# A graph network with a mixture-of-experts layer: all MLP units ahead of the matrix gather, row-major scans, output chunks loaded earlier, 36 columns by matmul in the last chunks

## The reference

```
x = x + gnn(layernorm(x))                       # 6250 nodes of 256, 200000 edges sorted by dst
    # relu(xn @ W + segment_sum((xn @ M)[src], dst))
x = x + ffn(layernorm(x))                       # 131072 edges, unsorted
    h      = x @ W_gat                          # 4 heads x 4 experts = 16 numbers per node
    e      = leaky_relu(a_src[src] + a_dst[dst])
    alpha  = exp(e - segment_max(e, dst)) / segment_sum(exp(...), dst)
    scores = layernorm(segment_sum(h[src] * alpha, dst) + b_gat).mean over heads
    w      = softmax(top 2 of the 4 scores), 0 for the others
    out    = sum over the 4 experts of w[e] * (gelu(x @ W1[e] + b1[e]) @ W2[e] + b2[e])
```

## Time and profile before

| what | before |
|---|---|
| time, median of 3 runs | 3039.76 us (3037.41 to 4880.14) |
| profiled execution, device time | 3039.66 us |
| its span, first to last instruction | 3038.4 us |
| mean granted TensorE clock | 0.921 of full |
| busy: PE, DVE, POOL | 2402.1, 2252.1, 2200.3 us |
| first stage, POOL's gathers | 63.8 to 2147.4 us, 1611 of them |
| second stage, POOL's gathers | 2188.8 to 2881.7 us, 512 of them |
| second stage, blocks picked | 2232.3 to 2871.1 us, 128 of them |
| POOL's last feature gather to the end | 155.7 us |

### The profile page before, as it was taken

The page is one execution under the profiler, slowest core; times in us unless marked ns, Lnnn a source line. Parts: engine busy times, 40 slices in busy tenths (PEclk is TensorE's granted clock), DMA queues, the critical chain, the costliest instruction groups (busy, mean ns, idle before and its releaser), DMA issues. The chain is left out here.

```text
span 3038.4 us, 42695 instructions
## 1 busy us (share of the span) xinstructions
PE 2402.1 (79%) x13244; PEld 1878.2 (62%) x13244; DVE 2252.1 (74%) x6360; ACT 541.7 (18%) x938; POOL 2200.3 (72%) x2260
## 2 busy tenths in 40 slices
PE   1466887878877878879888888988789999999723
PEld 0344565655655556557666666656579988888713
DVE  6589878877887656577666666666367999999958
ACT  4000121112112333322111111111100110011112
POOL 3677777777777777777777777777777777777760
PEclk9777998989999999989999999999899999999957
DMA  8977777777777777768877777877612222222188
GB/s 270 331 231 217 227 226 225 221 228 226 231 226 235 237 240 233 225 214 256 251 240 247 240 250 241 251 243 236 183 30 49 68 66 52 68 65 62 45 265 261
DMA packets 477160, 600.92 MB, mean 198 GB/s; under 512 B 72654, under 2 KB 415750, under 8 KB 474886
## 3 DMA queue, kind: packets, MB, share of 16 engines
q1 hardware_dynamic: 378886, 376.33, 37.6%
q0 software_dynamic: 97600, 220.02, 26.2%
q10 hardware_dynamic: 448, 1.85, 0.2%
HBM read 312.82 MB, written 286.79 MB: 197 GB/s over the span
## 5 line engine op out<-in xcount | busy, mean ns | idle before, releaser
L1544 POOL DMA_INDIRECT ring<-xn_d,srci x1611 | 1576.8, 979 | 514.5 <-issue 452.5
L776 DVE SCALAR_TENSOR_TENSOR ring<-ring,same_v,wide 128x256 f32<-128x256 f32 x1610 | 770.0, 478 | 564.1 <-PE wide L1352 460.0
L1352 PE MATMUL wide<-ring,one_hot 128*128 128x256 f32 x3222 | 916.5, 420 | 281.9 <-DMA ring<-xn_d,srci 171.4
L1352 PEld LDWEIGHTS wide<-ring,one_hot 128*128 128x128 f32 x3222 | 641.0, 208 | 514.6 <-DMA ring<-xn_d,srci 210.9
L1579 POOL DMA_INDIRECT g<-tab_d,srt x512 | 507.0, 990 | 156.1 <-issue 153.4
L1454 PE MATMUL wide<-tab_parts,low_hot 128*128 128x208 bf16 x6144 | 565.1, 253 | 50.3 <-DVE low_hot L818 50.2
L1454 PEld LDWEIGHTS wide<-tab_parts,low_hot 128*128 128x128 bf16 x6144 | 545.8, 98 | 71.2 <-DVE low_hot L818 63.4
L1410 PE MATMUL wide<-w2s,hh 128*128 128x256 f32 x1568 | 386.8, 391 | 1.5 <-DVE yo L754 1.5
L1400 PE MATMUL wide<-xt,w1s 128*128 128x512 f32 (+1 forms) x832 | 387.2, 589 | 0.8 <-DVE feat L744 0.8
L713 DVE TENSOR_SCALAR one_hot<-iota_f,dloc 128x128 f32<-128x128 f32 x1611 | 361.9, 304 | 3.2
L1157 ACT ACTIVATE hh<-wide,b1c 128x512 f32<-128x512 f32 (+1 forms) x208 | 137.9, 663 | 1215.7 <-PE wide L1400 1215.3
(11 more groups left out here) (359 smaller groups left out, 1444.2 us busy)
## 6 DMA issues: line engine op xcount, KB each, us to landing
run_d<-ring SPq DMA_DIRECT2D x201, 1024.0 KB, 5.3
ring<-xn_d,srci POOLq DMA_INDIRECT x1611
y_d<-yo SPq DMA_DIRECT2D x196, 128.0 KB, 2.6
comb<-y_d SPq DMA_DIRECT2D x28, 896.0 KB, 11.6
low_row<-low_d SPq DMA_DIRECT2D x16, 1024.0 KB
sum_d<-g SPq DMA_DIRECT2D x16, 768.0 KB, 3.9
g<-tab_d,srt POOLq DMA_INDIRECT x512
xn_d<-ring SPq DMA_DIRECT2D x7, 896.0 KB, 5.2
```

The lines of the kernel that those rows point to most:

```text
L776: dve_at["run", j] = step(V.scalar_tensor_tensor(out=o, in0=ring[:, (j - 1) // JC % RING, (j - 1) % JC, :], scalar=same_v[:, j:j + 1], in1 ...
L1352: T.matmul(wide[:, 4 + j // 2 % 2, j % 2 * D:(j % 2 + 1) * D], one_hot[:, j // 4 % 4, j % 4, :], ring[:, j // JC % RING, j % JC, :], start ...
L1544: G.indirect_dma_start(out=ring[:, s, j % JC, :], out_offset=None, in_=xn_d, in_offset=at_rows(srci[:, j:j + 1])).then_inc(sem(f"gather{s} ...
```

## The change

The diff has eight parts.

1. All of the 56 left units go ahead of the matrix steps: 8 of them (`GAP_UNITS`) into the first stage's loop at `gap_chunk` = 204, ahead of the turning of tile 48's sums, and 48 at the start of the second stage. The table is split between these units on DVE.
2. The last three chunks (13 to 15) have 36 columns by matmul and 28 by POOL: 131 blocks and 500 gathers instead of 128 and 512.
3. `weigh` and `sum_up` use row-major tiles: `by_row`, `logit`, `fade`, `reset_c`, each [128, rows, 65], column 0 of each row a restart value. One scan of 260 numbers makes all four maxima, five make the 20 sums. ACT copies the results back to `g` (six copies a chunk) before they are stored.
4. The end of the sort, one step before, is cut in five (`ENDS` = 4 more).
5. The zero stores and weight loads of c = 3 are spread: `run_d` at 3, `tab_d` at 4 and 5, `start_d` at 9 to 12, weights one at a time at 9 to 16.
6. Output chunk 0 and three of the loads of chunk 1 are loaded at matrix step 40; the rest of 1, and 2, after the last block is picked.
7. Part 1's gate stands ahead of output chunk 2's place in DVE's list; all seven tiles of chunk 2 are mixed by PE and ACT. Tiles by PE: 2, 2, 7, 3, 2, 3, 2 instead of 2 each.
8. The last store of sums is issued by ACT instead of SP.

```diff
+    gap_chunk = ready(NT - 1) + 3
+    units_at_visits, units_1 = units_1, units_1 + GAP_UNITS
-    turns_2, paced = ["unit"] * min(FIRST_UNITS, left), 0.0
-    (40 units spread over the matrix steps)
+    turns_2 = ["unit"] * left + ["matrix"] * matrix_total
...
 # PE, in the loop over c (ACT, DVE and SP likewise)
+            if c == gap_chunk:
+                for _ in range(GAP_UNITS):
+                    next(mlp)
             for k in due(c, 3):
                 turn_sums(k)
...
 # DVE, weigh(c)
-            for h in range(HEADS):
-                step(V.tensor_tensor_scan(g[:, s, :, FE + h], reset_c[:, c % 2, :], g[:, s, :, HX + h],
-                                          -BIG if c == 0 else before_top[:, :, h], ALU.add, ALU.max))
+            then(V.tensor_tensor(logit[:, :, now], g[:, s, :, HX:FE].rearrange("p k h -> p h k"),
+                                 a_dest.rearrange("p k h -> p h k"), ALU.add))
+            dve_at["topped", c] = then(V.tensor_tensor_scan(
+                flat(rows_top), flat(reset_c[:, :, :]), flat(logit[:, :, :]), 0.0, ALU.add, ALU.max))
 # DVE, sum_up(c)
-            for h in range(HEADS):
-                o = g[:, s, :, h * NX:(h + 1) * NX]
-                step(V.tensor_tensor(o, o, g[:, s, :, HX + h:HX + h + 1].broadcast_to([P, FC, NX]), ALU.mult))
-            for f in range(FE):
-                step(V.tensor_tensor_scan(g[:, s, :, f], st[:, :, h], g[:, s, :, f], ...))
+            for e in range(NX):
+                step(V.tensor_tensor(by_row[:, e * HEADS:(e + 1) * HEADS, now],
+                                     g[:, s, :, 0:HX].rearrange("p k (h e) -> p e h k", e=NX)[:, e, :, :],
+                                     rows_e[:, :, now], ALU.mult))
+            for e in range(NX + 1):
+                rows = flat(by_row[:, e * HEADS:(e + 1) * HEADS, :])
+                step(V.tensor_tensor_scan(rows, flat(fade[:, :, :]), rows, 0.0, ALU.mult, ALU.add))
...
 # SP, second stage
+            if done == PRELOAD:
+                (waits for x1_out, y_done, gelus, y_out)
+                for e in range(NX + 1):
+                    load_rows(0, e)
+                for e in range(EARLY_ROWS):
+                    load_rows(1, e)
...
 # DVE, output
-                if c * XG == t0:
+                if c == GATE_AT[part]:
                     gate(part, t0, t1)
-            s = c % CR
+            s, n = c % CR, XG - PE_TILES[c]
```

More of the change, by code:

```diff
@@ L311, in build @@
     PARTS = ((0, PART * XG), (PART * XG, NT))
+    first_mixed = [sum(PE_TILES[:c]) for c in range(NLN + 1)]
+    assert len(PE_TILES) == NLN and PE_TILES[PART - 1] == XG and GATE_AT == (0, PART - 1)
     FIX_PARTS = tuple((a, min(a + 512 // FG, NT)) for a in range(0, NT, 512 // FG))
-    ZERO_OUT = 16 * (FS + 3)
+    STARTS_ZERO, TABLE_ZERO = 16 * FS, 16 * 2
+    ZERO_AT, WEIGHTS_AT = 4, 9
+    GAP_UNITS = 8
     SHIFTED, SMALL, SCORES = 0, 64, 256
@@ L762, in vector_program @@
         for c in range(NCH + AFTER):
+            if c == gap_chunk:
+                for _ in range(units_1 - sum(late_after)):
+                    next(mlp)
             for k in due(c, 4):
@@ L788, in vector_program @@
                     norm_layer(k)
-        for _ in range(units_1 - sum(late_after)):
-            next(mlp)
         def split_table():
@@ L897, in weigh @@
+            then(V.tensor_tensor(logit[:, :, now], logit[:, :, now], rows_top[:, :, now], ALU.subtract))
+            dve_at["weighed", c] = then(V.tensor_scalar(fade[:, :, now], fade[:, :, now], 0.0, None, ALU.min))
             yield
@@ L938, in vector_program @@
         matrix_steps, chunks, done = matrix_gathers(), chunk_steps(), 0
-        for turn in turns_2:
+        table = split_table()
+        for i, turn in enumerate(turns_2):
             if turn == "unit":
                 next(mlp)
+                if 2 <= i:
+                    next(table, None)
                 continue
+            for _ in table:
+                pass
             next(matrix_steps)
@@ L1139, in sort_steps @@
                 yield
-            yield
+            for _ in range(ENDS + 1):
+                yield
             for t in range(NT):
@@ new lines, in scalar_program @@
+        for c in range(NLN):
+            if c == 0:
+                for _ in gate(0, *PARTS[0]):
+                    pass
+                A.wait_ge(dve_step, dve_at["gates", 0])
+            if c == PART:
+                A.wait_ge(dve_step, dve_at["gates", 1])
+            A.wait_ge(sem(f"comb_in{c % CR}"), 16 * (NX + 1) * (c // CR + 1))
+            tiles = range(XG - PE_TILES[c], XG)
+            if c == GATE_AT[1]:
+                second = gate(1, *PARTS[1])
+                for k in tiles:
+                    diagonals(c, k)
+                    if k in (2, 4, 6):
+                        next(second)
+                    if k >= 2:
+                        pour(c, k - 2)
+                for k in tiles[XG - 2:]:
+                    pour(c, k)
+                continue
+            for k in tiles:
+                diagonals(c, k)
+            for k in tiles:
+                pour(c, k)
@@ L1319, in sort_steps @@
                 yield
+            for _ in range(ENDS):
+                yield
             T.wait_ge(dve_step, dve_at["next"])
```

345 lines of the change are left out of this document (204 added, 141 removed).

## The result

| what | before | after |
|---|---|---|
| time, median of 4 runs | 3038.59 us (3036.72 to 3039.76, and one of 4880.14) | 3067.07 us (3056.04 to 3073.59) |
| profiled execution, device time | 3039.66 us | 3056.04 us |
| its span | 3038.4 us | 3054.8 us |
| last visit gather | 2147.4 us | 2129.0 us |
| first and last feature gather | 2188.8, 2881.7 us | 2186.9, 2865.7 us |

The ratio after to before is 1.0089, with a 95% interval of 1.0077 to 1.0102: the change makes the kernel 0.9% slower. 3034 was predicted, with a range of 3006 to 3057; the median lies 10 us above it. The execution of 4880.14 us is left out of the ratio, and no trace of it is kept. The profiled execution is the quickest of the four of after, so its trace explains 16.4 of the 28.5 us between the medians.

The account below looks back on a forecast made before the run. The prediction took POOL as the first stage's chain and DVE as the second stage's limit, with POOL close. From 3039.7 us, -14 + 21.4 + 0.3 - 13.0 = -5.3 gave 3034 us, range 3006 to 3057.

Parts of the forecast that it names:

- Spread stores and the cut sort: First stage: shorter POOL waits for the `run_d` store and the sort's last step, -14 us, bounds 0 and -14.7.
- The eight units: Between the stages: eight units ahead of tile 48 wait for `xt` and delay tile 48's features by 19.7 us.
- Rival B: Between the stages: `xt` lands early, tile 48 is not delayed, all of 19.7 goes: 3014 us; chance 0.08.
- Rival C: Second stage: POOL is the bound, with cheaper scans and full-rate column reads: 3017 us; chance 0.17.
- step "Blocks": Second stage: 131 blocks, 35.6 us a chunk including 1.0 for packed steps; scores of chunk 15 at 2903, +21.4 to L879.
- The row-major form: Chunk work on DVE: long scans save 3.1, column reads cost 0.9, restart columns 0.3: 13.5 becomes 11.6 us a chunk.
- DVE idle for PE for more than 2 us a chunk: Second stage, chunk steps: a sign that, if seen, would show the prediction wrong.
- products above 0.6: Chunk work on DVE: a sign that, if seen, would show the prediction wrong.
- step "Tail": After POOL's first tail gather: less mixing on DVE -11.8, part 1's gate wait +0.5, fewer loads -1.7: -13.0 us.
- From the logits to POOL's first tail gather: Stretch before the tail: scans and products -2.3, ACT's last copy +0.6, store beside seven loads +2: +0.3 us.
- D: Chunk work on DVE: dearer long scan (0.82) and column reads (0.3) make the kernel slower, 3058 us; chance 0.13.
- E: POOL stops as often as before, or the last store lands behind seven loads: 8 to 14 lost, 3046 us; chance 0.12.

Follow-up runs that it names:

- few_after2: Changed kernel with 1 feature gather a chunk by POOL, second run: 36.4 us a chunk, of it 1.9 DVE's wait for PE.
- few_unpack: Changed kernel with 1 feature gather a chunk and its row-major chunk work laid over 29 of 29 steps: 34.5 us a chunk.
- few_old_rows: Changed kernel with 1 feature gather a chunk and the chunk work of the kernel before, over 27 of 29 steps: 35.5 us a chunk.
- best: Changed kernel without units ahead of tile 48, most units among blocks, in-order products, chunk work over 29 steps, earlier x1 loads, other PE tiles: 4363.77 us, ratio 0.9916.
- best2: Kernel of best with tiles by PE 1, 1, 7, 3, 2, 3, 2: ratio to the kernel before 0.9892, on another chip 0.9920 (4310.60 us).
- old_rows: Changed kernel with the chunk work of the kernel before (24 scans of 64, no copies by ACT): 4406.96 us, ratio 1.0004 to the kernel before.
- start_only: Kernel before with only the spread zero stores and weight loads and the sort's end in five steps: 4394.26 us, ratio 0.9985.

## Why the prediction was wrong

**Right.** Spread stores and the cut sort: -14 predicted, -18.4 measured. POOL has no wait for `run_d` left in its first 400 us, where it had 9.0, and none above 0.3 between 900 and 1000. Over all visits its waits for `run_d` fell from 16.0 to 6.3 and those for DVE's running sums from 33.8 to 29.3, together 14.2; the other 4 us show in no wait, and in *after* all of this stands in one trace. The eight units: features +19.7 predicted. Relative to the last visit, POOL's first feature gather moved from 41.4 to 57.9 us, +16.5; on the other chips it lies 67 us (64 to 72, six runs) behind without the eight units and 87 (80 to 94, seven runs) with them (kernels with all their gathers). Rival B is out. Blocks start +42.1, against +42.9. Rival C is out: POOL ended 33 us ahead.

**Wrong, step "Blocks": packing, and DVE's own time.** A chunk takes 36.8, not 35.6. The trace of *after* splits this into 35.3 of DVE's own time, where my sum had 34.6, and 1.5 of waiting for PE, where I took 1.0 for the packing. Without the gathers packing costs even 1.9 (few_after2 against few_unpack), more than my bound of 1.7. Of the 3.5 x 1.1 = 3.9 us that DVE has to spare in the steps without chunk work, I counted on 2.9 to be saved by the two buffers; 1.9 to 2.4 are. The two errors are 0.5 + 0.7 = 1.2 us a chunk, 18 us in 15 chunks. The ledger lacks only 14.8, since I had counted 15.2 chunks up to the scores of chunk 15, where there are 15 (-6), and the first scores stand 96.4 us behind the first block and not 94 (+2). My own sign for it, DVE idle for PE for more than 2 us a chunk, stayed silent; the other, products above 0.6, came true.

**Within DVE's own time.** The row-major form was to save 13.5 - 11.6 = 1.9 and saves 1.0 (few_old_rows against few_unpack). A column read costs 0.71 - 0.355 = 0.36 more per instruction, not 0.18: 1.8 a chunk, not 0.9. I had taken the price from a reduction in steps of 16 bytes, and the steps here are of 96: 0.7 ns an element there, 1.4 here. The Trainium skill (SBUF — State Buffer, section Door 1: The DMA port swizzle) says that every new 16-byte line pays. The trace agrees that such reads pay, and the old products, four in a line, did not: 416 ns, as L903 over `step_f` in order, 0.42 us. The Trainium skill gives no size. A scan of 260 costs 0.61, close to the 0.65 taken, and six give 0.2 back; the last 0.2 of the 0.9 that are missing is not traced. Against this, the units that left the blocks free 0.7 a chunk and not the 0.4 of their bias adds. So 0.9 - 0.3 = 0.6 of the 0.7 is accounted for. POOL's gathers cost DVE 0.7 a chunk in both kernels: in my sum they hid in the 13.5 of chunk work, harmlessly.

**Wrong, step "Tail".** -13.0 predicted, -2.4 measured. DVE's mixing got shorter by 8.4 and 3.2, as told, and its first gate came 2.9 earlier. But the wait for part 1's last sums is 4.6 and not 0.5: with the earlier gate DVE stood there 64.4 us after POOL's first tail gather, and the last of 49 gathers, at 1.29 each, starts at 63.1 and lands 6 later, at 69. In the trace of before it lands 68.7 us behind the first, and I had 67.5. I booked the earlier first gate as a gain and did not see that DVE would only wait longer for the same sums. The x1 wait of 4.9 has no term in my sum. I held that "DVE never waited for a chunk in its 25.22 and 33.63", which was true of the old order: now chunk 2, mixed by PE and ACT among the gate's own steps, is out only at 3010.2, 25 us behind chunk 1 (2984.7), SP waits for it, and chunk 5's load of x1 stands behind it. In *best* and *best2* SP issues it ahead of that store, and the wait is gone. The end of the last chunk by PE and ACT comes 2.6 later. 4.1 + 4.9 + 2.6 less the 1.2 by which the first gate beat its forecast of 1.7 is 10.4 of the 10.6 that are missing.

**Wrong by a little.** From the logits to POOL's first tail gather +1.8, not +0.3. With the old scans in the same place it is 19.6 (old_rows), with the old store 17.3 (start_only): the store that runs beside seven loads costs 2.3, as I took it (2), but the row-major form gives back only 0.5 at this place. From the logits to the end of the scans DVE takes 10.2 instead of 11.8, 1.6 less and not 2.3, and the store stands 1.1 behind that for ACT's last copy, 1.0 more than before where I took 0.6.

**Two readings that were wrong without effect.** L870's scans, which I called contiguous, go through `edge` in steps of 16 bytes. And POOL stops at a third place in the first stage, 6.8 us for `srci`; it does so in both traces.

**Rivals D and E** had the sign. D had half of the reason: reading columns is dearer than it said (0.36, it had 0.3), but the long scan is cheap, and laid out evenly the row-major form still saves 1.0 a chunk. E looked for POOL's waits and the last store; it had no part in it.

**Open.** The executions of after lie between 3056 and 3074, those of before between 3037 and 3040 but for the one of 4880. The other 12 us between profile and medians have no trace. A gain of the spread units alone was not shown either, only that of *best2* as a whole.

## What to carry to other kernels

Work that becomes shorter must also lie in the right places: when one engine sets the pace in some steps and another in the rest, count each step's maximum, not the sum over a chunk, and lay shortened work out again over the freed steps. When an output chunk is moved to slower engines, look through the queue that issues its store for loads of other chunks that stand behind it. When work ahead of a wait gets shorter, ask whether what is waited for comes any earlier; if not, nothing is gained. Before moving units ahead of a stage, ask what they delay: here 42 us on the chain bought 0.7 us a chunk.
